# Gated cross-attention block with a quantised feed-forward: maxima of |h| taken two tiles at a time, the last pair one chunk later

## What is computed

```python
def _act_fake_quant(x, clip_factor):
    scale = jax.nn.sigmoid(clip_factor) * jnp.max(jnp.abs(x)) / QMAX
    return jnp.clip(_ste_round(x / scale), -QMAX - 1.0, QMAX) * scale

xq = _act_fake_quant(x, clip_x[0])
gate = jnp.einsum('bsh,ih->bsi', xq, _weight_fake_quant(w_gate))
up = jnp.einsum('bsh,ih->bsi', xq, _weight_fake_quant(w_up))
h = _act_fake_quant(jax.nn.silu(gate) * up, clip_down[0])
return jnp.einsum('bsi,hi->bsh', h, _weight_fake_quant(w_down))
```

## Time and profile before

| | us |
|---|---|
| median of three runs | 288.77 |
| the profiled execution | 288.73 |
| its span, first to last instruction | 286.9 |
| VectorE busy | 214.0 (75%) |
| TensorE busy, matmul | 233.8 (81%) |
| ScalarE busy | 175.2 (61%) |
| GpSimd busy | 126.1 (44%) |
| gate/up stage, first matmul to the reduction over `h_max` | 227.05 to 259.41 |

### The profile page before, as it was taken

One profiled execution on the slowest core, in us unless ns is written; L12 is line 12 of the kernel. 1 busy time (PEld: TensorE's weight loads), 2 busy tenths in 40 slices (PEclk: granted clock), 3 DMA queues, 4 the chain that ended last, 5 costly groups with the idle time before them and its releaser, 6 DMA issues.

```text
span 286.9 us, 6295 instructions
## 1 busy us (share of the span) xinstructions
PE 233.8 (81%) x1784; PEld 156.9 (55%) x1788; DVE 214.0 (75%) x463; ACT 175.2 (61%) x326; POOL 126.1 (44%) x203
## 2 busy tenths in 40 slices
PE   0699987989878999999999899999961498853990
PEld 1577766767745675666566575755640233322660
DVE  3479888775576868796988969799427469997991
ACT  1325476375686766676666757676961388865940
POOL 3375655533262313637353453737524144430462
PEclk9999999999999999999999999999999589995796
DMA  7829799973335554424355553100000700000298
GB/s 231 244 52 333 231 295 287 257 187 113 110 110 114 111 113 98 98 75 102 78 111 110 112 111 75 38 1 1 2 2 3 256 0 3 0 0 0 29 127 140
DMA packets 31638, 31.28 MB, mean 109 GB/s; under 512 B 5248, under 2 KB 28288, under 8 KB 31616
## 3 DMA queue, kind: packets, MB, share of 16 engines
q1 hardware_dynamic: 26832, 27.87, 37.5%
q0 software_dynamic: 1904, 1.84, 4.9%
q10 hardware_dynamic: 2880, 1.31, 1.8%
HBM read 20.65 MB, written 10.22 MB: 108 GB/s over the span
## 4 chain that ended last, share of the span: by engine, by line
PE 44%; DVE 20%; issue 12%; ACT 7%; DMA 7%; POOL 4%; SPq 3%; DVEq 1%; POOLq 1%; ACTq 0%
PE bank_o L1290 7%; PE bank_a L1273 6%; PE bank_b L1260 5%; PE bank_m L1316 5%; DMA x_rows<-in_x 4%; DVE neg_max L801 4%; PE bank_a L1182 4%; PE bank_o L1193 3%; PE bank_b L1413 3%; PE bank_m L1298 2%; ACT big L658 2%; DVE arena L1085 2%; DMA qk_parts<-arena 2%; DVE h_max L1045 2%; PE bank_a L1413 2%
## 5 line engine op out<-in xcount | busy, mean ns | idle before, releaser
L801 DVE TENSOR_REDUCE neg_max<-bank_b 128x2 f32<-128x512 f32 x112 | 73.3, 680 | 11.3 <-PE bank_b L1260 11.0
L658 ACT ACTIVATE big<-bank_a 128x512 f32<-128x512 f32 x128 | 69.6, 589 | 15.5 <-PE bank_a L1273 14.8
L1273 PE MATMUL bank_a<-big 98*128 98x256 bf16 x256 | 49.0, 274 | 3.1 <-DVE neg_max L801 0.9
L1260 PE MATMUL bank_b<-big 96*128 96x256 bf16 x224 | 42.8, 272 | 0.0
L1290 PE MATMUL bank_o<-big,v_cur 128*32 128x256 f32 x512 | 34.3, 385 | 0.8 <-ACT big L658 0.8
L1182 PE MATMUL bank_a<-arena,w_t 128*128 128x256 f32 x128 | 30.3, 385 | 0.6 <-DVE resid L812 0.5
L477 POOL CAST max_parts<-max_f 8x256 bf16<-8x256 f32 x16 | 6.5, 403 | 52.6 <-issue 51.2
L1273 PEld LDWEIGHTS bank_a<-big 98*128 98x128 bf16 x256 | 21.1, 97 | 13.5 <-ACT big L658 3.6
L450 POOL TENSOR_TENSOR arena<-resid,arena 128x512 bf16<-128x512 f32 x16 | 18.4, 1160 | 18.8 <-ACT arena L597 18.8
L1182 PEld LDWEIGHTS bank_a<-arena,w_t 128*128 128x128 f32 x128 | 23.8, 194 | 4.0 <-DVE resid L812 1.1
L1260 PEld LDWEIGHTS bank_b<-big 96*128 96x128 bf16 x224 | 21.5, 97 | 3.2 <-issue 0.2
(11 more groups left out here) (160 smaller groups left out, 456.9 us busy)
## 6 DMA issues: line engine op xcount, KB each, us to landing
qk_parts<-arena SPq DMA_DIRECT2D x8, 768.0 KB, 4.6
big<-qk_parts SPq DMA_DIRECT2D x32, 192.0 KB, 3.6
big<-qk_parts SPq DMA_DIRECT2D x32, 128.0 KB, 3.9
x_rows<-in_x SPq DMA_DIRECT2D x8, 256.0 KB, 5.4
big<-qk_parts SPq DMA_DIRECT2D x32, 64.0 KB, 3.9
out<-x_rows SPq DMA_DIRECT2D x8, 256.0 KB, 3.1
big<-in_ctx SPq DMA_DIRECT2D x7, 256.0 KB, 6.1
out<-v_all POOLq DMA_DIRECT2D x7, 256.0 KB, 4.7
```

The costliest lines, as they stand in the source:

```text
L658: act.activation(p_buf[:, h % HH], bank_a[:, h % 2].rearrange("p (c s) -> p c s", c=QC), ACT.Exp, scale=SCALE).then_inc(exp_done, 1)
L801: dve.tensor_reduce(neg_max[:, p, :, h], bank.rearrange("p (c s) -> p c s", c=QC), axis=AX.X, op=ALU.max, negate=True).then_inc(max_done, 1)
L1260: done = mm(to, q_st[0:KR, p, h, c * P:(c + 1) * P], k_st[0:KR, p, h], start=True, stop=not masked)
L1273: done = mm(to, k_st[0:KM, p, h, k * P:(k + 1) * P], q_st[0:KM, p, h], start=True, stop=not masked)
```

## The change

The maxima are taken in pairs of tiles by one instruction each, which reads 2 x 512 elements of each partition and writes two columns of `h_max`. The pairs are tiles (0, 2), (1, 3) and (4, 5). The second pair stands behind product 5, the first behind product 3. The pair (4, 5), which waits for GpSimd's last product of the chunk, stands behind product 2 of the next chunk; that of the last chunk stands at the end. Chunks 0 and 1 are now written out on VectorE like the others, so their waits need no registers. Nothing is changed on the other engines.

```diff
@@ -1016,7 +1016,7 @@
             def quantise(n, a):
 
                 dve.wait_ge(xq_tr, n)
-                if isinstance(n, int):
+                if n == 1:
                     dve.wait_ge(x_over_scale, 1)
                 else:
                     dve.wait_ge(pool_x, n - 1)
@@ -1036,39 +1036,40 @@
-            def h_maximum(n, c):
-                r, u = (P if c < IC - 1 else ILAST), n * IC + c
-                if c in POOL_CHUNKS:
-                    dve.wait_ge(pool_h_done, 2 * n + c // 3 + 2)
-                else:
-                    dve.wait_ge(h_done, 4 * n + DVE_CHUNKS.index(c) + 3)
-                chain.then(dve.tensor_reduce(h_max[0:r, tile(u)], h_all[0:r, c, bass.ds(n * CW, CW)], axis=AX.X, op=ALU.max,
+            MAX_PAIRS = ((0, 2), (1, 3), (4, 5))
+
+            def h_maxima(n, pair):
+                c, d = MAX_PAIRS[pair]
+                for m in (c, d):
+                    if m in POOL_CHUNKS:
+                        dve.wait_ge(pool_h_done, 2 * n + m // 3 + 2)
+                    else:
+                        dve.wait_ge(h_done, 4 * n + DVE_CHUNKS.index(m) + 3)
+                chain.then(dve.tensor_reduce(h_max[:, bass.ds(n * IC + 2 * pair, 2)],
+                                             h_all[:, c:d + 1:d - c, bass.ds(n * CW, CW)], axis=AX.X, op=ALU.max,
                                              apply_absolute_value=True))
 
             def products(n, ahead=False):
 
-                for c, maxima_of in zip(DVE_CHUNKS, ((), (0,), (2, 1), (3,))):
+                for c, pair in zip(DVE_CHUNKS, (None, 2, 0, 1)):
...
-                    for m in maxima_of:
-                        h_maximum(n, m)
+                    if pair == 2 and n:
+                        h_maxima(n - 1, 2)
+                    elif pair in (0, 1):
+                        h_maxima(n, pair)
                     if ahead and c == 3:
                         quantise(n + 2, n)
                     if ahead and c == IC - 1:
                         clip()
-                h_maximum(n, IC - 1)
-                h_maximum(n, 4)
-
-            with dve.Fori(0, 2) as n:
-                chain.loop(n, IC + 1)
-                products(n, ahead=True)
-            chain.end(2)
-            products(2)
-            products(3)
+
+            for n in range(NCH):
+                products(n, ahead=n < 2)
+            h_maxima(NCH - 1, 2)
             chain.wait()
```

## The result

The changed kernel takes 290.15 us (median of 14 runs, 288.83 to 291.9). The kernel before takes 287.89 us in 14 runs beside it (287.25 to 290.21). The ratio, that of the means, is 1.0064, with a 95% interval of 1.0034 to 1.0094 (the medians are 2.3 us apart). It is slower, by 0.64% or about 1.9 us, which is within 1%, and its 290.15 us are inside the forecast range. The forecast said slower by 0.5 us. The sign was right and the size was not: most of the loss has a cause that the forecast does not name.

The account below looks back on a forecast made before the run. VectorE was taken to bound the stage. From 288.73 us, gaps added 1.3, pairs saved 0.6 (together +0.7), and 0.2 came off for earlier ScalarE work and cheaper waits: +0.5, forecast 289.2 us, range 287.6 to 290.4.

Parts of the forecast that it names:

- the forecast's plus sign: VectorE's stage: idle gaps grow from 1.3 to 2.60 us, more than the pairs' 0.6 us gain; slower by 0.5 us.
- What bounds the stage: VectorE, busy 7.21 of 7.24 us in chunk 1, sets the stage; its last three maxima precede the reduction over `h_max`.
- Part 1, the price of a pair: VectorE's maxima: a pair lasts 1210 ns, costs 1.13 us start to start against 1.18 for two; twelve gain 0.6 us.
- Part 2, the walk through the new order: VectorE's program stepped through with silu times held: the reduction over `h_max` starts at 260.09 us, 0.68 later.
- "0.5 us later is still early enough": Clip on VectorE: its delay is harmless because the transpose behind it is needed only after tile 2.
- The deduction of 0.2: Chunk 1 onward: ScalarE's earlier work shrinks later gaps and waits without registers may cost less; -0.2 us for both.
- The rival "GpSimd is kept out": Tile 4 products, chunks 0 to 2: pairs stop GpSimd, up to 1.2 us each, 3.6 in all, 292.8 us; chance 0.04.
- The rival "the lead pays": Chunks 1 to 3: other engines come earlier with product 0, 1.37 us of gaps vanish, 288.0 us; 0.28 including cheaper pairs.

Follow-up runs that it names:

- e2: The changed kernel with quantise moved ahead of the pair (0, 2), directly behind product 3; ratio to the kernel before 1.0074.
- e3: The changed kernel with quantise directly behind product 3 and clip directly behind product 5, both ahead of the pairs; ratio to the kernel before 1.0011.
- e1: The kernel before with VectorE's chunks 0 and 1 written out instead of looped, nothing else; ratio to the kernel before 1.0028.
- e4: The changed kernel with the pair (4, 5) at the end of its own chunk instead of behind product 2 of the next; ratio to the kernel before 1.0104.
- e7: The changed kernel with GpSimd's product of tile 4 of chunk 1 cut to 32 of 512 elements; one run, 292.36 us, not compared.
- e5: The changed kernel with pairs (0, 1), (2, 3), (4, 5) placed into VectorE's waits, quantise behind product 3, clip behind product 5; 287.14 us, ratio to before 0.9947.
- e8: The same kernel as e2, run once more; ratio to the kernel before 1.0017.
- e6: The changed kernel's order with each pair of maxima as two instructions of one tile; ratio to the kernel before 1.0066.

## Why the prediction was right, and where it was not

The sign and the range came true in part by luck. The forecast had gaps that outweigh the gain of the pairs by 0.7 us, and took 0.2 off. Measured, D rose by 1.70 us. The held-up quantise makes 1.25 us (changed kernel to e2) and the place of clip 0.75 (e2 to e3), together 2.00, and without these two the kernel is 0.30 us below before (e3). So the mechanism behind the forecast's plus sign is not what made the kernel slower. And the range was laid around 288.8 us: 0.64% on 288.77 would be 290.6 us, just above it, but the kernel before took 287.89 in the later runs.

**What bounds the stage** held: the reduction over `h_max` waits for VectorE's last maxima in every kernel.

**Part 1, the price of a pair,** held. The forecast of 1210 ns for 1024 elements met 1204 ns, in VectorE's groups by form of the changed kernel, and a start-to-start distance of 1.13 us (258.74 with two in 2.33 us). Against singles in the same order the pairs gave 0.29 us of D, where the sum had 0.6; part of the gain is eaten by waits that others set.

```profile
L1048 DVE TENSOR_REDUCE h_max<-big 128x2 f32<-128x1024 f32 x12 | 14.4, 1204 | 0.0
L1023 DVE TENSOR_SCALAR arena<-arena 128x1024 bf16<-128x1024 f32 x3 | 3.0, 989 | 1.2 <-PE bank_m L1397 1.2
```

**Part 2, the walk through the new order,** held to 0.1 us from product 3 of chunk 0 to the middle of chunk 1 (product 2 of chunk 0 came 0.56 us earlier than in the walk, for the reason given under TensorE's clock below). From silu to product it took 0.10 us (233.35 to 233.45) where the walk had 0.14; the forecast had allowed for that. The walk failed at one term, which it took over from the kernel before whatever GpSimd does beside it: quantise at 0.59 and clip at 0.34 us from start to start in both chunks. The second row above shows what came, a mean of 989 ns where two of three took 0.69 or less. Quantise of chunk 1 cost 1.51 from start to start (242.77 to 244.28), 0.92 more than its term, and clip 0.36 more than its own. The forecast put the end of clip of chunk 1 at 245.38 + 0.43 = 245.81; it came at 246.97.

**"0.5 us later is still early enough"** is the step that made this into time. In the kernel before clip of chunk 1 ended at 245.12 and the transposes started at 245.97; in e1 it was 244.24 and 245.09. So the slack was 0.85 us. The forecast used up 0.69 of it (245.81 less 245.12), and the collision took 1.16 more. TensorE itself was ready 0.21 us earlier than before, at 245.76, and waited 1.26 us. The step fails even without the collision: in e2 clip ended 12.27 us behind product 3 of chunk 0 (the forecast had 12.35), but TensorE was ready at 11.95, where it had been 12.51 before, and waited 0.38. The lead of product 0 had reached TensorE, and so the slack was gone. In the changed kernel everything from product 2 of chunk 2 on is 0.8 to 1.1 us later than forecast: 247.55 against 246.71 there, 258.08 against 257.05 at product 5 of chunk 3, and 261.10 against 260.09 at the reduction. By the walk D was 260.09 - 233.46 = 26.63, measured 27.65; the 1.02 us between them is this chain. The deduction of 0.2 for a ScalarE that comes earlier took it from +0.7 to +0.5 and could not show as long as clip was late.

**The rival "GpSimd is kept out"** looked at the right resource with the wrong partner. Pairs never touched GpSimd: in the changed kernel seven of its eight products last 1.26 or 1.27 us, and the one of 1.49 stood beside quantise, not beside a pair. I had read in the earlier trace rows that quantise made GpSimd wait, and had used it only to clear the pairs. The trace also says that the product of 242.64 and quantise, 242.73, start within a tenth of a microsecond, so any shift of VectorE's order can turn the meeting round. That belonged into the sum as a rival of its own.

**The rival "the lead pays"** failed in the changed kernel and is seen in e3, where clip is early: there D is 25.65, 0.98 below the walk's 26.63. Of this rival's 1.37 us of gaps about 0.8 close; the one ahead of product 2 of chunk 3 stays, at 0.45 of its 0.48. The rest is that clip no longer waits for the end of a pair, 0.12 in each of two chunks. So whether the lead pays was decided by the places of quantise and clip, one instruction of VectorE away each.

**How the time follows D.** The changed kernel's D is 1.70 us longer and its time 1.9 us, by the ratio. In the two runs of one kernel the ratios differ by 0.57%, so I don't account for the remainder. Nor does D decide a single time: the rest of the span, outside D, takes 260.1 to 261.0 us in eight of the ten traces, and 262.5 in e4 and 263.6 in e7, though the program is the same there.

## What to carry to other kernels

In a stage where VectorE is full and GpSimd works beside it, list those instructions of VectorE that were seen to collide (here quantise and clip) with GpSimd's products on one time line, and ask after each move which of them starts first. Here the order of two engines at one point was worth 1.25 us and the twelve instructions saved 0.3. An instruction that another engine waits for, such as clip, belongs directly behind its last input, and long work that nobody needs soon, such as a maximum, into the waits. A walk through the program with durations from rows, with that term in it, named the D of every experiment: five lie in the stated range (e1, e2, e3, e5, e7), and so does the repeat e8, and the other two miss theirs by 0.13 (e4) and 0.06 us (e6).

## What the runs showed of the hardware

**Of quantise or clip and a product of GpSimd, one keeps the other waiting, in both directions.** With quantise started 0.22 or 0.32 us ahead of the product (235.31 and 235.53 before the change; 235.25 and 235.57 after) the product grows by 0.33 and 0.23 us. With quantise 0.09 us behind the product's start the product still takes the wait: 1.89 us (before, and e1). With quantise 0.22 us or 0.34 us behind, quantise takes it: 1.59 (changed) and 1.47 us (e6). So it is not strictly the first to start that wins; the turn lies somewhere between 0.09 and 0.22 us. In each case the loser's excess is the time from its start to the winner's end less 0.13 to 0.15 us: quantise of 242.77 had 1.04 us of the product ahead of it and grew by 0.91. Clip does the same: 0.50 us left, 0.36 more (changed), and 0.76 left, 0.61 more (e7). An overlap of 0.11 us (clip at 247.51 and the product of 247.83 in e4) cost nothing. Maxima and products of VectorE showed no such effect beside any product of GpSimd: pairs took 1.20 to 1.22 us throughout. The Trainium skill, in "GPSIMD Engine Reference", section "Specifications", names VectorE instructions in a two-port mode or with two SBUF inputs as those that contend for the interfaces that GpSimd shares. The trace agrees as far as it goes: quantise takes 0.68 us for 1024 elements and collides, a pair takes 1.20 us for as many and does not. In which mode an instruction ran the trace does not record.

**TensorE's clock moves the start of the stage.** From product 0 to product 3 of chunk 0 it took 4.67 us in the kernel before, 5.34 in the changed one and 5.02 to 5.50 in the others. The stage begins at the lower of the clock's two levels, 1.2 GHz of 2.4: the granted clock is 0.50 of full speed in its first microseconds, after TensorE had been idle for 3.04 and 1.87 us with only eight transposes between. Over the stretch of the changed kernel that holds most of chunk 0 it is 0.79 on average, and 1.00 in chunk 1 (start:end, length, busy us of PE, PEld, DVE, ACT and POOL, clock, DMA):

```profile
228.50:229.50 1.00, 1.00 (x3) 0.30 (x2) 0.36 (x1) 0.51 (x1) 0.00 (x0) 0.50 0.00 0
227.05:238.32 11.27, 10.14 (x42) 4.23 (x41) 6.19 (x8) 7.81 (x12) 3.86 (x3) 0.79 0.06 21
238.32:246.88 8.56, 6.35 (x33) 2.49 (x32) 8.39 (x10) 6.61 (x11) 3.80 (x3) 1.00 0.01 3
```

The eight transposes behind tile 2 of chunk 0 take 0.61 us at a granted clock of 1.00 in the kernel before and 0.89 at 0.68 in the changed one, so in the former the clock had risen by then. I left this part out of D for that reason. That the order on VectorE has an influence on it is not shown: before and e1, which have the same order, differ by 0.35 us there.
